# Up-projection of a feed-forward layer by Strassen's seven products, with the other weights streamed through four slots

## The chip, the cores and the metric

The kernel runs on one core of one Trainium2 chip. The metric is the device time of one execution in microseconds (us). TensorE is called PE here, VectorE DVE, ScalarE ACT, GpSimd POOL and the queue of DMA issues on SyncE SP. All arithmetic is fp32; a product of two fp32 matrices is made of three matmuls on a high and a low part of each operand.

## The reference

```python
# x: (32, 128, 512); ctx: (32, 128, 512)
x = x + tanh(g_xattn) * xattn(layernorm(x), ctx)   # 16 heads of 32, k and v from ctx
h = layernorm(x)                                   # 4096 rows of 512
u = square(relu(h @ up_w))                         # up_w: (512, 2048)
s = u @ down_w                                     # down_w: (2048, 512)
r = top_k(h @ gate_w, 2).sum(-1, keepdims=True)    # gate_w: (512, 8)
y = s + (h @ expert_w) * r                         # expert_w: (512, 512)
x = x + tanh(g_ffn) * (norm(y) * gamma + beta)
```

The first layer (attention) is left as it is, but for its last steps; the change is in the second (feed-forward).

## The kernel before

**Tiles.** A row tile is 128 rows of x. After the attention the 32 tiles lie in the DRAM scratch `x2_scratch`. The feed-forward layer takes them in eight groups of four (512 rows); group 0 and group 7 are written out, groups 1 to 6 are the body of one hardware loop (`run`, L1116), with the same order of instructions on each engine in every turn. Nothing plans the order: each engine runs its list in order, and semaphores that only count up (`at_least`) hold it back.

**Splitting.** ACT copies an fp32 tile into a float32r tile (the high part) and DVE or POOL subtracts it from the source (the low part). `mm3` (L68) then issues hi×hi, hi×lo and lo×hi for each of the stationary 128x128 blocks.

**A group.** For each of the 16 output tiles of 128 columns of `up_w`, `upward` (L990) issues 12 matmuls with 512 moving columns (4 blocks of the contraction, 3 each) into bank 4 or 5. ACT takes relu (L1281), DVE squares (L1320), ACT makes the high part (L1272), DVE the low part (L1322), and `downward` (L1220) issues 12 matmuls with 512 moving columns, which add into banks 0 to 3 (`wide`). PE's order is upward(i), downward(i-1). Then come four `expert` products (L1232) of 12 matmuls. `gate` (L1199) and `turn_logits` (L1209) make the routing weights early in the group.

**Weights.** All weights of the layer (up, down, expert) are split once, in group 0, and stay in SBUF. Their tiles carry the names of the attention's weights that lay in the same place: `wk` holds the turned x of the group, `wq` and `up` the up weights, `wv` and `down` the down weights, `wo` the expert weights.

**Turning x.** PE needs x with its 512 features on the partitions. From group 1 on, DVE normalises a tile (L1034), and `deal_blocks` (L1162, on SP) stores it to `xn_scratch` with one DMA (L1164), waits until that has landed, and reads it back with four DMAs (L1169) that permute 32x32 blocks, in pieces of 128 bytes. DVE then transposes inside the blocks (`turn_blocks`, L1010), and ACT and DVE split the result (L1008, L1039). Four tiles a group are so dealt with, each as soon as it is normalised.

**Around it.** `load_x` (L958) fetches the next group's tiles, `finish` (L1182) the residuals and stores the results. The attention's `drain` functions (L253, L396, L578, L739, L863) interleave the last attention tiles with the start of group 0, and `keep_clock` (L339) issues matmuls whose result is not used.

Of the kernel before, what the change touches and what calls it, by code (L numbers as in the profile page):

```python
# [5 lines left out]
F32 = mybir.dt.float32  # L6
# [5 lines left out]
P = 128  # L12
# [11 lines left out]
def flamingo_layer(nc, t, out):  # L24
# [10 lines left out]
    xn_dram = nc.dram_tensor("xn_scratch", [GB, P, D], F32, kind="Internal").ap()  # L35
# [11 lines left out]
    with ExitStack() as whole:  # L47
# [35 lines left out]
        fy = sb(whole, "fy", [P, GB, D])  # L83
        st_x2 = [sem(f"st_x2_{n}") for n in range(2)]
        dv_x2, pe_V = sem("dv_x2"), sem("pe_V")
        ff = feed_forward_start(nc, whole, t, x2_dram, bank, ident, tanh_g, powers, W, fx, fy, at_least, mm3)
# [4 lines left out]
        with ExitStack() as ctx:  # L91
            bk = sb(ctx, "bk", [P, D])
            bq = sb(ctx, "bq", [P, D])
            bv = sb(ctx, "bv", [P, D])
            tgbo = sb(ctx, "tgbo", [P, D])
            nqk = sb(ctx, "nqk", [P, D])
            xin = [sb(ctx, f"xin{n}", [P, D]) for n in range(2)]
            cin = [sb(ctx, f"cin{n}", [P, D]) for n in range(2)]
            xres = [sb(ctx, f"xres{n}", [P, D]) for n in range(2)]
            x2 = [sb(ctx, f"x2_{n}", [P, D]) for n in range(2)]  # L100
            xn = sb(ctx, "xn", [P, D])
            xnT_hi, xnT_lo = sb(ctx, "xnT_hi", [P, D], F32R), sb(ctx, "xnT_lo", [P, D], F32R)
            cT_hi = [sb(ctx, f"cT_hi{n}", [P, D], F32R) for n in range(2)]
            cT_lo = [sb(ctx, f"cT_lo{n}", [P, D], F32R) for n in range(2)]
            kb, qb, vb = sb(ctx, "kb", [P, D]), sb(ctx, "qb", [P, D]), sb(ctx, "vb", [P, D])
            kf, qf = sb(ctx, "kf", [P, D]), sb(ctx, "qf", [P, D])
            junk_k, junk_q = sb(ctx, "junk_k", [P, D]), sb(ctx, "junk_q", [P, D])
            v_hi = [sb(ctx, f"v_hi{n}", [P, D], F32R) for n in range(2)]
            v_lo = [sb(ctx, f"v_lo{n}", [P, D], F32R) for n in range(2)]
            qT_hi, qT_lo = sb(ctx, "qT_hi", [P, D], F32R), sb(ctx, "qT_lo", [P, D], F32R)  # L110
# [4 lines left out]
            pT_hi, pT_lo = sb(ctx, "pT_hi", [P, NG, HG * P], F32R), sb(ctx, "pT_lo", [P, NG, HG * P], F32R)  # L115
            aT = sb(ctx, "aT", [P, NG, P])
# [30 lines left out]
            BO_LAST = bank[6]  # L147
# [54 lines left out]
            def _(sp):  # L202
# [50 lines left out]
                def drain(s, a, o):  # L253
# [5 lines left out]
                    ff.load_piece(sp, ff.nstage)  # L259
                    sp.wait_ge(dv_x2, a + 1)  # L260
                    sp.dma_start(x2_dram[a], x2[a % 2][:, :]).then_inc(st_x2[a % 2], DMA)
                    for m in range(ff.nstage + 1, 2 * ff.nstage):
                        ff.load_piece(sp, m)
# [6 lines left out]
            def _(pe):  # L270
# [125 lines left out]
                def drain(s, a, o):  # L396
# [6 lines left out]
                    ff.turn(pe, 0)  # L403
# [4 lines left out]
                    ff.turn(pe, 1)  # L408
# [3 lines left out]
                    ff.turn(pe, 2)  # L412
                    keep_clock(BO_LAST, 8, 2 * P)
                    keep_clock(BO_LAST, 8, 2 * ff.NE)
                    project_out(a, BO_LAST)
                    turn_probs(s, s % 2, 2)
                    turn_probs(s, s % 2, 3)
                    ff.turn(pe, 3)
                    for g in range(NG):
                        values(s, s % 2, g)  # L420
                    ff.upward(pe, 0, 0)
                    ff.upward(pe, 0, 1)
                    pe.wait_ge(dv_x2, a + 1)
                    project_out(s, BO_LAST)
# [4 lines left out]
            def _(dve):  # L429
# [148 lines left out]
                def drain(s, a, o):  # L578
# [13 lines left out]
                    ff.lo_T(dve, 0, 1)  # L592
                    split_values(a)
# [3 lines left out]
                    ff.piece_lo(dve, 0)  # L597
# [3 lines left out]
                    ff.lo_T(dve, 0, 3)  # L601
                    residual_sum(a, a % 2, BO_LAST)
                    ff.piece_lo(dve, 1)
                    ff.piece_lo(dve, 2)
                    split_values(s)
                    ff.prepare(dve)
                    residual_sum(s, s % 2, BO_LAST)
# [4 lines left out]
            def _(act):  # L612
# [71 lines left out]
                def slot(s, par):  # L684
# [50 lines left out]
                    if is_slot(s, 0):  # L735
                        for k in range(KT):
                            weight_hi(3, k)

                def drain(s, a, o):  # L739
                    hi_v(s, s % 2)  # L740
                    exps(s, s % 2, 0)
                    exps(s, s % 2, 1)
# [737 lines left out]
```

## Time and profile before

| | |
|---|---|
| median of 3 runs | 1479.23 us (1478.67 to 1479.96) |
| the profiled execution | 1478.99 us |
| its span, first to last instruction | 1476.8 us |
| busy: PE, PEld, DVE, ACT, POOL | 98%, 79%, 59%, 46%, 31% |
| mean granted TensorE clock | 0.995 |

The span leaves out what lies before the first and after the last instruction, 2.2 us here. PE is the matmuls, PEld the loads of their stationary operand, which run beside them. A matmul's record is longer than the step to the next one, since matmuls overlap in the array: what a matmul costs is read from the distance of two starts, not from its duration. SPq is SP's queue of DMA issues: a row's time is the time that issuing takes, and the landing of the data comes later. In the timeline, merged rows (x2, x4) run from the start of the first to the end of the last.

### The profile page before, as it was taken

The numbers are of one execution on the slowest core, as the hardware profiler recorded it, in microseconds if no ns is written. First come the engines' busy times: TensorE is split into PE (matmuls) and PEld (weight loads), VectorE is DVE, ScalarE is ACT, GpSimd is POOL, SyncE is SP. The second block draws the span as 40 slices with busy tenths as digits, with TensorE's granted clock in tenths as the row PEclk, the third lists the DMA queues.
The fourth block names the chain that finished last, engine by engine and source line by source line (L and its number), as shares of the span: only waits on it lengthen the run. The fifth ranks groups of instructions, "written<-read, shape, count | busy, mean of one in ns | idle before, by whom it ended". The sixth has DMA issues, their size and how long they took to land.

```text
span 1476.8 us, 24473 instructions
## 1 busy us (share of the span) xinstructions
PE 1444.6 (98%) x7984; PEld 1169.9 (79%) x7984; DVE 869.9 (59%) x1495; ACT 685.8 (46%) x1951; POOL 456.3 (31%) x587
## 2 busy tenths in 40 slices
PE   6899999999999999999999999999999999999997
PEld 4688888888888888778878878788788788788786
DVE  5677777787777788655554353353453443543524
ACT  3677777777777777744322222222222222222221
POOL 2555555555555557600020020020020110200211
PEclk9999999999999999999999999999999999999999
DMA  6121111111111131033411301202211212112000
GB/s 215 44 58 57 57 57 57 57 57 57 55 54 54 51 122 50 30 114 111 124 51 43 87 28 43 71 28 51 63 43 43 64 43 50 56 43 57 36 22 29
DMA packets 103559, 89.74 MB, mean 61 GB/s; under 512 B 64480, under 2 KB 64608, under 8 KB 103520
## 3 DMA queue, kind: packets, MB, share of 16 engines
q1 hardware_dynamic: 102944, 88.19, 20.0%
q10 hardware_dynamic: 576, 1.05, 0.2%
q8 instruction: 22, 0.36, 0.1%
q14 instruction: 17, 0.14, 0.0%
HBM read 65.10 MB, written 24.12 MB: 60 GB/s over the span
## 4 chain that ended last, share of the span: by engine, by line
PE 93%; DVE 2%; POOL 2%; ACT 1%; issue 1%; DMA 1%; SPq 0%; POOLq 0%; DVEq 0%; ACTq 0%
PE bank L74 18%; PE bank L76 17%; PE bank L75 17%; PE wide L74 10%; PE wide L75 10%; PE wide L76 10%; PE bank L324 3%; PE wide L302 3%; PE bank L285 3%; POOL prob L804 1%; ACT prob L636 1%; DMA prob<-in_wk 1%; PE bank L1216 1%; PE bank L1206 0%; PE bank L1203 0%
## 5 line engine op out<-in xcount | busy, mean ns | idle before, releaser
L1281 ACT ACTIVATE relu<-bank 128x512 f32<-128x512 f32 x128 | 76.5, 597 | 420.9 <-PE bank L76 420.9
L1320 DVE TENSOR_TENSOR hid<-relu 128x512 f32<-128x512 f32 x128 | 98.1, 766 | 265.2 <-ACT relu L1281 265.1
L636 ACT ACTIVATE prob<-wide,nmx 128x128 f32<-128x128 f32 x512 | 182.0, 404 | 19.1 <-DVE nmx L458 19.1
L804 POOL TENSOR_TENSOR prob<-prob,rr 128x512 f32<-128x512 f32 x128 | 137.8, 1087 | 88.4 <-DVE rr L466 88.4
L76 PE MATMUL bank<-wk_hi,up_lo 128*128 128x512 f32 x384 | 152.0, 396 | 0.0
L75 PE MATMUL wide<-down_lo,hT_hi 128*128 128x512 f32 x384 | 151.7, 395 | 0.0
L75 PE MATMUL bank<-wk_lo,up_hi 128*128 128x512 f32 x384 | 151.6, 395 | 0.0
L74 PE MATMUL bank<-wk_hi,up_hi 128*128 128x512 f32 x384 | 151.6, 395 | 0.0
L74 PE MATMUL wide<-down_hi,hT_hi 128*128 128x512 f32 x384 | 151.6, 395 | 0.0
L76 PE MATMUL wide<-down_hi,hT_lo 128*128 128x512 f32 x384 | 151.4, 394 | 0.0
L1322 DVE TENSOR_TENSOR hT_lo<-hid,hT_hi 128x512 fp32r<-128x512 f32 x128 | 89.4, 698 | 89.8 <-ACT hT_hi L1272 89.8
L1272 ACT ACTIVATE hT_hi<-hid 128x512 fp32r<-128x512 f32 x128 | 80.9, 632 | 124.1 <-DVE hid L1320 124.1
L636 ACT ACTIVATION_READ_ACCUMULATOR prob<-wide,nmx 128x1 f32 x512 | 125.0, 244 | 0.0
L1067 POOL TENSOR_SCALAR fvar<-fmv 128x1 f32<-128x1 f32 x32 | 7.2, 224 | 332.2 <-DVE fmv L1030 332.2
L1404 POOL TENSOR_TENSOR fres<-fres,beta 128x512 f32<-128x512 f32 x32 | 42.9, 1345 | 179.9 <-DMA fres<-x_scratch 179.9
L614 ACT ACTIVATE aT<-wide 32x512 f32<-32x512 f32 x128 | 75.5, 590 | 42.5 <-PE wide L76 41.0
L614 ACT ACTIVATE pT_hi<-bank 128x512 fp32r<-128x512 f32 x128 | 72.3, 671 | 36.3 <-PE bank L324 36.3
L1398 POOL TENSOR_SCALAR yvar<-ymv 128x1 f32<-128x1 f32 x32 | 15.8, 494 | 227.7 <-DVE ymv L1343 227.7
L75 PEld LDWEIGHTS wide<-down_lo,hT_hi 128*128 128x128 f32 x384 | 72.1, 188 | 17.6
L74 PEld LDWEIGHTS wide<-down_hi,hT_hi 128*128 128x128 f32 x384 | 72.1, 188 | 17.4
L76 PEld LDWEIGHTS wide<-down_hi,hT_lo 128*128 128x128 f32 x384 | 72.1, 188 | 17.4
L75 PEld LDWEIGHTS bank<-wk_lo,up_hi 128*128 128x128 f32 x384 | 72.1, 188 | 17.3
(162 smaller groups left out, 3612.6 us busy)
## 6 DMA issues: line engine op xcount, KB each, us to landing
xin<-in_x SPq DMA_DIRECT2D x32, 256.0 KB, 2.6
cin<-in_ctxT SPq DMA_DIRECT2D x32, 256.0 KB, 2.9
xres<-in_x SPq DMA_DIRECT2D x32, 256.0 KB, 3.5
x_scratch<-x SPq DMA_DIRECT2D x32, 256.0 KB, 2.9
fx<-x_scratch SPq DMA_DIRECT2D x32, 256.0 KB, 2.7
fres<-x_scratch SPq DMA_DIRECT2D x32, 256.0 KB, 3.6
out_x<-fres SPq DMA_DIRECT2D x32, 256.0 KB, 2.0
xn_scratch<-fx SPq DMA_DIRECT2D x28, 256.0 KB, 2.0
```

The source lines that it names most:

```text
L74: eng.matmul(dst, ah, bh, start=first and k == 0, stop=False)
L75: eng.matmul(dst, ah, bl, start=False, stop=False)
L76: mm = eng.matmul(dst, al, bh, start=False, stop=last and k == n - 1)
L285: mm = pe.transpose(cols(dst, k), cols(src, k), ident[:, :])
L302: mm = pe.matmul(cols(bank[g], h), cols(q, h)[strip(g), :], kT[strip(g), m, h, :], start=n == 0, stop=n == 2)
L614: return act.activation(dst, src, ACT.Copy)
L636: i = act.activation(prob[par][:, g, h * P:(h + 1) * P], cols(bank[g], h), ACT.Exp, bias=nmx[:, n:n + 1], scale=1.0, accum_out=rs[:, n:n + 1])
L804: pool.tensor_tensor(p, p, r, ALU.mult).then_inc(po_p, 1)
L1272: return act.activation(dst, src, ACT.Copy)
L1281: act.activation(ff.relu[:, :], bank[4 + i % 2], ACT.Relu).then_inc(ff.ac_r, 1)
L1320: dve.tensor_tensor(ff.hid[:, :], ff.relu[:, :], ff.relu[:, :], ALU.mult).then_inc(ff.dv_h, 1)
L1322: dve.tensor_tensor(ff.hT_lo[i % 2][:, :], ff.hid[:, :], ff.hT_hi[i % 2][:, :].bitcast(F32), ALU.subtract).then_inc(ff.dv_l, 1)
```

## The change

Two output tiles of `up_w` (a pair q of eight) and the group's 512 rows are seen as 2x2 blocks of 256x256 and 256 rows. Strassen's scheme (Winograd's form) gives the 2x2 product with seven half-size products in place of eight. Each of the seven is 6 matmuls with 256 moving columns (2 blocks of the contraction, 3 each). Their operands are sums and differences of blocks: of the weights, made once in group 0 by POOL (`up_sums`), and of the normalised x, made in each group by POOL (`x_sums`) as four more tiles "t" beside the four of x. So eight tiles are dealt, turned and split per group and not four. DVE puts the products together (`sum_2`, `sums_all`: seven operations of 256 columns a pair) and squares with one operation a tile (`squares`); relu on ACT is gone, two copies of 256 columns a pair come in.

The seven sums of up weights take 1.75 times their old room, so the down and expert weights no longer stay in SBUF: group 0 splits them and stores both parts (512 KB a tile) to `ring_scratch`, and groups 1 to 7 read them back through four slots. PE takes the slots in the order down 0 to 13, expert 0 to 3, down 14, 15 ("places" 0 to 19); the expert product now runs one contraction block at a time over banks 4 to 7. A slot is loaded again only when the downward or expert step four places before has ended (`pe_R`).

The core of the diff:

```diff
+    def product(pe, q, b, half, a, moving):
+        stat = [tuple(w[q][:, a * H + kk * P:a * H + (kk + 1) * P] for w in (u_hi, u_lo)) for kk in range(2)]
+        mm3(pe, bank[b][:, half * H:(half + 1) * H], stat, moving).then_inc(pe_P, 1)
-        mm3(pe, bank[4 + i % 2], [tuple(w[:, k * P:(k + 1) * P] for w in up[i]) for k in range(KT)],
-            [(xT_hi[:, k, :], xT_lo[:, k, :]) for k in range(KT)]).then_inc(pe_U, 1)
+        at_least(pe, dv_U, n * NC)                      # upward(g, q): seven products
+        product(pe, q, 4, 0, 0, [x_part(kk, 0) for kk in range(2)])
...
+        at_least(pe, ac_P, n * 2 + 1)
+        product(pe, q, 4, 1, 1, [x_part(2 + kk, 0) for kk in range(2)])
+        at_least(pe, dv_U, n * NC + 1)
+        product(pe, q, 5, 1, 5, [t_part(2, kk) for kk in range(2)])
...
+        def ring_ready(g, n):
+            if is_first(g):
+                pe.wait_ge(ff.rl, n + 1)
+            else:
+                per = NS // KT * 2 * DMA
+                at_least(pe, ff.ring_moved[n % KT], g * per + (n // KT + 1) * 2 * DMA)
...
         def group(g):                                   # PE
+            for q in range(NQ):
+                if not (is_first(g) and q == 0):
+                    ff.upward(pe, g, q, (lambda: turn_logits(g)) if q == 1 else None)
+                if q == 0:
...
+                else:
+                    downward(g, 2 * q - 2)
+                    downward(g, 2 * q - 1)
+            if not is_last(g):
+                experts(g)
+            downward(g, NI - 2)
+            downward(g, NI - 1)
...
+        def ring_load(g, n, last=False):                # SP
+            at_least(sp, ff.pe_R, g * NS + (n - KT + 1), apart=True)
+            i = n if last else ff.ring_order[n]
+            for m in range(2):
+                sp.dma_start(ff.ring[n % KT][m].bitcast(F32), ring_dram[i, m]).then_inc(ff.ring_moved[n % KT], DMA)
+        def out_blocks(g, i):
...
+            sp.dma_start(xn_dram[i], src).then_inc(ff.st_n[ff.pair_of(i)], DMA)
+        def in_blocks(g, i):
+            dst_tile = ff.y[i] if i < GB else ff.xn[i - GB]
+            at_least(sp, ff.st_n[ff.pair_of(i)], g * (2 * DMA), apart=True)
+            src = xn_dram[i].rearrange("(c t) (k i d) -> i t k c d", t=HD, k=KT, d=HD)
+            for m in range(HG):
+                dst = dst_tile[m * HD:(m + 1) * HD, :].rearrange("t (k c d) -> t k c d", k=KT, d=HD)
+                sp.dma_start(dst, src[m]).then_inc(ff.ld_t[ff.pair_of(i)], DMA)
...
         def group(g):                                   # SP, for q in range(NQ)
+                if not first and q in (2, 3):
+                    store_out(g - 1, q - 2)
+                    load_res(g - 1, q)
+                if not first and q == 4:
+                    store_out(g - 1, 2)
+                if not first and q > 0 and 2 * q + 2 < (NI if last else NS):
+                    ring_load(g, 2 * q + 2, last)
+                if not last and q in (6, 7):
+                    jj = q - 6
+                    out_blocks(g + 1, 2 * jj)
+                    out_blocks(g + 1, 2 * jj + 1)
+                    out_blocks(g + 1, GB + jj)
+                    out_blocks(g + 1, GB + jj + 2)
+                    in_blocks(g + 1, 2 * jj)
+                    in_blocks(g + 1, 2 * jj + 1)
+                if not first and q > 0 and 2 * q + 3 < (NI if last else NS):
+                    ring_load(g, 2 * q + 3, last)
+                if not last and q in (6, 7):
+                    jj = q - 6
+                    in_blocks(g + 1, GB + jj)
+                    in_blocks(g + 1, GB + jj + 2)
+                if not first and q == 4:
+                    store_out(g - 1, 3)
...
+            elif not last:
+                for n in range(2 * NQ + 2, NS):
+                    ring_load(g, n)
+            if not last:
+                for n in range(KT):
+                    ring_load(g + 1, n)
...
+    def x_sums(pool, g, jj, t_tiles):                   # POOL, into the tiles y
+        at_least(pool, dv_xn, g * GB + 2 * (jj + 1), apart=True)
+        pool.tensor_tensor(ta[:, 0:H], xb[:, 0:H], xa[:, 0:H], ALU.subtract).then_inc(po_t, 1)
...
+            ff.inv_std(pool, g + 1, 1)                  # POOL's group(g)
+            next_sums(g, 0)                             # waits until all four results are stored
+            ff.inv_std(pool, g + 1, 2)
```

In group 0 the ring is filled by DMA, ACT and DVE: SP stores each split tile and then loads the next piece to be split, in the same places of its list as the ring loads above. In the last group nothing is dealt, and the expert weights are read into the place of up weights that are used up. In the drain of the attention eight tiles are transposed by PE in place of four, POOL makes the first sums, and the two `keep_clock` calls there are gone.

## Rows read from the trace of the kernel before

**Rows 1.** The page: span, busy times, chain of waits that ended last

```profile
span 1476.8 us, 24473 instructions
PE 1444.6 (98%) x7984; PEld 1169.9 (79%) x7984; DVE 869.9 (59%) x1495; ACT 685.8 (46%) x1951; POOL 456.3 (31%) x587
PE 93%; DVE 2%; POOL 2%; ACT 1%; issue 1%; DMA 1%; SPq 0%; POOLq 0%; DVEq 0%; ACTq 0%
```

**Rows 2.** Windows (us, busy of each engine with instructions, clock): one group, gate to gate

```profile
850.40:953.70 103.30, 103.30 (x450) 82.74 (x449) 45.65 (x78) 24.99 (x41) 14.13 (x20) 1.00 0.18 51
```

**Rows 3.** Waits of PE from 650 us to the end

```profile
PE bank L74 <- issue: 0.7, 2, 0.3
```

**Rows 4.** Timeline of PE, 512 moving columns (start us, duration us), the first and last of 13

```profile
1001.36 0.39 PE L74 MATMUL bank<-wk_hi,up_hi 128*128 128x512 f32 x1
...
1004.14 0.40 PE L74 MATMUL wide<-down_hi,hT_hi 128*128 128x512 f32 x1
```

**Rows 5.** Timeline of PE, 256 moving columns, read in narrow windows

```profile
627.42 0.40 PE L342 MATMUL bank<-cT_hi 128*128 128x256 f32 x2
627.54 0.40 PE L342 MATMUL bank<-cT_hi 128*128 128x256 f32 x2
627.66 0.40 PE L342 MATMUL bank<-cT_hi 128*128 128x256 f32 x2
```

**Rows 6.** Timeline of PE and PEld: transposes in groups of four, each behind a wait

```profile
625.76 1.04 PE L324 MATMUL bank<-ident,prob 128*128 128x128 f32 x8
626.63 0.60 PE L982 MATMUL bank<-ident,fx 128*128 128x128 f32 x4
625.53 1.02 PEld L324 LDWEIGHTS bank<-ident,prob 128*128 128x128 f32 x8
1001.13 0.19 PEld L74 LDWEIGHTS bank<-wk_hi,up_hi 128*128 128x128 f32 x1
```

**Rows 7.** Timeline of SP's issues: a tile dealt out and in; residual loads

```profile
893.18 0.33 SPq L1164 DMA_DIRECT2D xn_scratch<-fx  x1
895.26 2.64 SPq L1169 DMA_DIRECT2D fx<-xn_scratch  x4
946.71 2.15 SPq L1185 DMA_DIRECT2D fres<-x_scratch  x4
```

**Rows 8.** DMA issues of one group (count, KB each, median us from issue to landing)

```profile
xn_scratch<-fx SPq DMA_DIRECT2D x4, 256.0 KB, 2.0
fx<-xn_scratch SPq DMA_DIRECT2D x16, 64.0 KB, 2.5
fx<-x_scratch SPq DMA_DIRECT2D x4, 256.0 KB, 2.9
fres<-x_scratch SPq DMA_DIRECT2D x4, 256.0 KB, 4.0
```

**Rows 9.** Groups of DVE, ACT and POOL in one group of tiles (busy us, mean ns | idle before)

```profile
L1320 DVE TENSOR_TENSOR hid<-relu 128x512 f32<-128x512 f32 x16 | 12.3, 769 | 33.6 <-ACT relu L1281 33.6
L1322 DVE TENSOR_TENSOR hT_lo<-hid,hT_hi 128x512 fp32r<-128x512 f32 x16 | 11.1, 692 | 11.3 <-ACT hT_hi L1272 11.3
L1034 DVE TENSOR_SCALAR fx<-fx,fmv,frstd 128x512 f32<-128x512 f32 x4 | 2.2, 541 | 0.0
L1281 ACT ACTIVATE relu<-bank 128x512 f32<-128x512 f32 x16 | 9.6, 598 | 55.5 <-PE bank L76 55.5
L1404 POOL TENSOR_TENSOR fres<-fres,beta 128x512 f32<-128x512 f32 x4 | 5.6, 1407 | 27.2 <-DMA fres<-x_scratch 27.2
```

**Rows 10.** Windows behind PE's last matmul; timeline of PE at half clock

```profile
1468.00:1472.00 4.00, 0.51 (x3) 0.09 (x1) 3.83 (x8) 0.69 (x1) 2.04 (x3) 1.00 0.32 123
1472.00:1476.80 4.80, 0.00 (x0) 0.00 (x0) 1.78 (x3) 0.00 (x0) 1.36 (x2) 0.55 0.28 109
13.18 0.63 PE L75 MATMUL bank<-wk_lo,cT_hi 128*128 128x512 f32 x1
13.61 0.63 PE L76 MATMUL bank<-wk_hi,cT_lo 128*128 128x512 f32 x1
```

**Rows 11.** Waits of PE from 613 to 650 us, the change from attention to group 0

```profile
PE wide L74 <- DVE hT_lo L1322: 1.2, 1, 1.2
PE bank L74 <- DVE aT_lo L431: 0.8, 1, 0.8
PE bank L324 <- DVE pT_lo L431: 0.5, 1, 0.5
PE wide L74 <- ACT prob L636: 0.5, 1, 0.5
```

More of the change, by code:

```diff
@@ L1220, in downward @@
         def downward(g, i):
-            if static(g) and g == 0:
-                pe.wait_ge(ff.fl, ff.have("down", i))
+            n = spot(g, i)
+            ring_ready(g, n)
             at_least(pe, ff.dv_l, g * NI + (i + 1))
@@ L1245, in group @@
[L1245 to L1265 removed]
+                pe.wait_ge(ff.ld_e, KT * 2 * DMA)
@@ L1312, in _, with evict @@
-        run(act, group, before)
+            at_least(act, ff.pe_R, (g + 1) * NS - 2)
+            act.activation(ff.y[j], bank[4 + j], ACT.Copy, scale=route[:, j:j + 1]).then_inc(ff.ac_m, 1)
+        def evict(g, j):
+            at_least(act, ff.pe_R, g * NS + NI)
+            at_least(act, ff.st_o[j], g * DMA)
+            copy(ff.y[j], bank[j]).then_inc(ff.ac_m, 1)
+        def group(g):
+            first, last = is_first(g), is_last(g)
+            for q in range(NQ):
+                if q > 1:
+                    hidden_hi(g, 2 * q - 2)
+                    hidden_hi(g, 2 * q - 1)
+                if q == 1:
+                    logits(g)
+                if first and q == 1:
+                    freed(act)
+                if not (first and q == 0):
+                    ff.copy_1(act, g, q)
+                    ff.copy_5(act, g, q)
+                if q == 1:
+                    hidden_hi(g, 0)
+                    hidden_hi(g, 1)
+                if first and q + 2 < NQ:
+                    if q == 1:
+                        freed(act)
+                        stored(act)
+                    ff.up_hi(act, q + 2, 0)
+                    ff.up_hi(act, q + 2, 1)
+                if first:
+                    if q + 2 < NQ:
+                        ff.up_hi(act, q + 2, 2)
+                    ring_hi(2 * q)
+                    ring_hi(2 * q + 1)
+            hidden_hi(g, NI - 2)
+            hidden_hi(g, NI - 1)
+            if last:
+                for j in range(GB):
+                    evict(g, j)
+                return
+            if first:
+                ring_hi(2 * NQ)
+                ring_hi(2 * NQ + 1)
+            for i in range(GB):
+                ff.hi_T(act, g + 1, i)
+            if first:
+                ring_hi(2 * NQ + 2)
+                ring_hi(2 * NQ + 3)
+            ff.hi_T(act, g + 1, GB)
+            ff.hi_T(act, g + 1, GB + 1)
+            weigh(g, 0)
+            ff.hi_T(act, g + 1, GB + 2)
+            weigh(g, 1)
+            ff.hi_T(act, g + 1, GB + 3)
+            weigh(g, 2)
+            weigh(g, 3)
@@ L1427, in after @@
                 scale_y(NGRP - 1, j)
-        run(pool, group, before, after)
+        run(pool, group, None, after)
 def kernel(**inputs):
```

980 lines of the change are left out of this document (646 added, 334 removed).

## The prediction

> **What bounds the kernel now.** I read the page first: PE is busy 98% of the span and carries 93% of the chain that ended last, with DVE at 59% and ACT at 46% [rows 1]. Then I cut out one feed-forward group, from gate to gate. PE is busy for the whole 103.3 us at full clock, DVE for 45.7, ACT for 25.0 and POOL for 14.1 [rows 2], and from 650 us to the end PE waits only 0.7 us [rows 3]. So the layer is a stream of matmuls, and what counts is the step from one to the next and whether anything new interrupts it. With 512 moving columns 12 steps take 2.78 us, 0.232 us each [rows 4]. A group is 440 such matmuls (384 up and down, 48 expert, 8 gate), 102.1 us, and the small ones of the logits. A steady group is thus 103.3 us, and eight are 826 of the 1477 us.
>
> **The matmuls.** The only place that shows 256 moving columns with a new 128x128 stationary block each is a keep-clock burst: starts at 627.42, 627.54, 627.66, 0.120 us apart [rows 5]. A pair of output tiles took 24 x 0.232 = 5.57 us and now takes 42 x 0.120 = 5.04 us. Strassen removes one eighth of the columns, 0.70 us, but 1.75 times as many loads and starts give 0.17 back. Over 8 pairs and 8 groups the gain is 64 x 0.53 = 34 us. Bounds: the transposes, 128 columns with full weight loads, step by 0.109 us (eight of them and the four behind them start 0.87 us apart) [rows 6], so 0.109 is a floor (gain 64 x 0.99 = 63). The records of the loads are 0.19 us long but start closer than that, so 0.19 isn't the step. A ceiling is half of 0.232 plus the excess of a 512 step over 512 columns at 2.4 GHz (0.232 - 0.213 = 0.019), 0.126 (gain 18). I take the burst's 0.120, as it is the same shape. The seven waits of a pair cost nothing when already met: the transposes in rows 6 are groups of four, each behind a wait, without a break.
>
> By the Trainium skill (TensorE: Matmul & The Clock Gate, sections "Back-to-back issue gap" and "LDWEIGHTS") a warm matmul takes 262 cycles at 256 columns and 518 at 512, and a load of 128 columns about 107 ns whatever streams beside it. The trace agrees on the load's floor (0.109) and shows 0.016 more at 512 columns and 0.011 more at 256. By the page's steps the gain would be 64 x (24 x 0.216 - 42 x 0.109), an estimate of 39 us, and a further halving of the columns would gain nothing, since the load would be the step.
>
> **DVE and ACT within a pair.** At 512 columns DVE takes 0.69 to 0.77, ACT 0.60 from PSUM [rows 9]. For 256 columns I halve the part that grows with columns and get 0.42 on DVE and 0.4 on ACT (bounds 0.35 and 0.69, 0.30 and 0.60). DVE adds 7 x 0.42 = 2.9 us a pair, and four more turned tiles a group (transpose 0.7, low part 0.7) 5.6 us: 46 + 24 + 6 = 76 of some 99 us. PE's period is 5.04 + 5.57 = 10.6 us a pair. DVE must hand over the sums within the 5.57 us of the two downwards: from the last product two sums (0.8 us) if it isn't behind. The hidden tiles are needed 10.6 us after the product: two squares, high and low parts, about 4 us. Hidden. ACT loses 16 relus (9.6 us) and gains 16 copies of 256 (6.6 us) and four copies of turned tiles; it is idle three quarters of the group. Nothing.
>
> **One wait that POOL brings.** next_sums(g, 0) needs the four results of the group before stored, and the last store is issued behind ring load 11, so behind downward 7, the end of pair 4. From there: ring load 0.95, store landing 2.0 to 3 [rows 8], four half-width POOL operations 2.8 (half of 1.41 each [rows 9]), the inverse deviation of the third tile, queued behind them on POOL, 0.8, then on DVE normalise 0.54, statistics 1.0 and six sums 2.5. That is 10.6 to 11.9 us, against 10.6 us until PE wants bank 4. DVE's sums of pair 5 stand behind that normalise, and PE behind the sums. 0 to 2.5 us a group; I take 1.3, six times: 8 us.
>
> **The queue of SP at the turn of a group.** Here I expect the result to be decided. Before, four tiles were dealt, each by itself when it was normalised, and nothing that PE needed soon was queued behind them. A deal is 0.33 us of issue, a landing 2.08 us after its start, and four issues of strided DMAs in 2.64 us, 0.67 from start to start; these land 2.5 us after issue [rows 7, 8]. Now eight tiles are dealt in pairs 6 and 7, in one list with ring loads of 512 KB that PE needs within this stretch. Count from the end of downward 10, before which SP may not issue ring load 14, and so nothing behind it. PE, if never held, runs downward 11 (2.78), pair 7 (5.04), downwards 12 and 13 (5.57), expert 0 to 2 (8.35): expert 3, which reads ring load 17, would start at 21.7 us. Before load 17 has been issued SP must issue:
> - 24 strided DMAs (six tiles in) at 0.67 and six waits at 0.15: 17.0 us
> - 16 plain DMAs (loads 14 to 17, eight tiles out) at 0.45, between the 0.33 of a bare one and the 0.6 of those in the loop (four in 2.15 [rows 7]): 7.2 us
> - twice the wait for a landing, 2.08 and 0.5 for the ring load ahead of it, less the 1.3 us in which two more tiles go out: 2.5 us
>
> Together 26.7 us, and the load lands 2.9 us later [rows 8], at 29.6: expert 3 is 7.9 us late (1 us of it already at expert 2). It ends at 32.4. Behind load 17 stand two more tiles in (5.7 us) and load 18 (0.95), which lands at 36.2: downward 14 is another 3.8 us late. Load 19 follows by 0.95 and is hidden by downward 14. Sum 11.7 us. PE's clock: behind its last matmul (1468.5 us) the clock is full until 1472 and 0.55 in the next window; at the start of the kernel matmuls at 1.2 GHz step by 0.43 us [rows 10]. An idle time of 7.9 us is longer than those 4 us, so expert 3 would run at half clock, 2.3 us longer, nearly all inside the wait for load 18. I take 12 us a turn. Bounds: with 0.38 and 0.66 us an issue, no cost for waits, and landings of 2.0 us, load 17 lands at 26.2 and the sum is 7.6 us; with 0.6 and 0.73 and landings of 4 us [rows 8] it is 18.
>
> It would not help to have only the ring right: the last tile in is issued at 32.5 us and lands at 35, then transpose 0.7, high 0.6, low 0.7 make 37, while an undisturbed PE would want the t tiles at 30 + 2.2 = 32. Both chains come from the same list. Six turns (groups 1 to 6): 72 us.
>
> **Group 0.** Its turn has the same eight tiles, but between them SP stores split tiles and loads raw ones that ACT and DVE must still split. All eight deals stand ahead of the load for place 18: the two steps with their stores and loads come to about 37 us, landing 3, split 1.4: downward 14 at 41 against 24.5, and 1 us more behind it in load 19. 17 us (bounds 11 and 22, the spread of the other turns scaled).
>
> **The rest.** In the drain 16 more transposes (1.7 us) and POOL's sums, against two keep-clock bursts (1.7 us) gone and PE waits of 3.0 us there now [rows 11]: +2 (between -3 and +6). The tail after the last matmul keeps its shape: 0. Drained and loaded weights in other groups: ring loads 4 to 13 have over 15 us each, 0.
>
> **Sum**, against the profiled execution's 1479.0 us (span 1476.8 and 2.2 around it; the median of the runs is 0.2 higher): 1479.0 - 34 + 8 + 72 + 17 + 2 = 1544 us. All low ends together give 1479 - 63 + 0 + 46 + 11 - 3 = 1470, all high ends 1479 - 18 + 15 + 108 + 22 + 6 = 1612; they won't fall together, and the likeliest case's own range is 1502 to 1580.
>
> **Rivals.**
> 1. The list of SP is not in the way: stores and strided issues overlap more than rows 7 show, and the turn costs at most what POOL's and DVE's chain costs. For it: SP is hardly used in the rest of the group, PE has four slots ahead, and a reader of rows 3 sees that the old deals held nobody. Against: SP's starts 0.67 apart are in the trace, inside the same loop. Then 1479 - 34 + 2 + some 3 = 1450, faster. It decides from a stall of under 4.9 us a turn (34 over 7). 11%.
> 2. The stall is there but small, 4 to 5.5 us a turn (the plain DMAs cheap, E3 alone late): 1479 - 34 + 7 x 4.75 + 2 = 1480, between 1475 and 1502. 7%.
> 3. The half-width step isn't 0.120: the load, 0.19 us by its record, becomes the step when it meets a wait or a fresh bank. 42 x 0.19 = 8.0 us a pair, 64 x 2.4 = 154 us more than now, and with longer pairs the turn's stall falls to some 9 us: 1479 + 154 + 63 = 1696. The burst and the transposes speak against it. 2%.
> 4. The change doesn't do what it says: PE gains nothing since the products' seven waits break the stream (the step behind a real wait is about 0.1 us longer): 64 x 7 x 0.08 = 36 us, the gain is gone: 1580. Within the upper end; 5%.
>
> **Chances.** Likeliest case 75%. The range 1490 to 1575 leaves out rivals 1 and 3, most of rival 2 and part of rival 4, some 2 in 10. A measurement tells 0.2%, 3 us, from no change: faster 0.12 (rival 1 and a part of 2), same 0.01, slower 0.87.
>
> **What would show it.** PE steps of 0.120 in the seven products (right: 0.118 to 0.126). In each group from 1 to 6 two idle times of PE, some 7 us ahead of the third or fourth expert block and some 4 ahead of downward 14, both released by the DMA of the ring; SP's queue without a hole from downward 10 to there, mostly strided issues; the clock at half right behind the longer one. Group 0 longer than the others by 5 us at its turn. A wait of about 1 us ahead of pair 6, ended by DVE. Wrong, if the groups are 99 us long, if PE's waits at the turn are ended by DVE's low parts of x alone, or if the steps are 0.19.

## The result, and the profile of the changed kernel

The changed kernel takes 1613.06 us, the median of 4 runs (1611.13 to 1616.2), against 1479.6 of the kernel before beside it (1478.67 to 1480.04): a ratio of 1.0905, 95% interval 1.0885 to 1.0924. Forecast were 1544 us in a range of 1490 to 1575. The sign and the places are as predicted; the time is outside the range. The profiled execution took 1616.2 us, 3 above the median.

Its span is 1614.4 us. Three lines of the page (busy times, clock in 40 slices, chain of waits), against [rows 1]:

```profile
PE 1464.2 (91%) x9136; PEld 1236.7 (77%) x9136; DVE 1090.9 (68%) x2003; ACT 679.8 (42%) x1991; POOL 557.8 (35%) x691
...
PEclk9999999999999999888799899899899899898999
...
PE 65%; SPq 12%; DMA 8%; DVE 7%; issue 4%; POOL 3%; ACT 1%; POOLq 0%; DVEq 0%; ACTq 0%
```

SP's queue and the DMAs now hold 20% of the chain that ended last, where they held 1%. PEclk falls to 8 and 7 in four slices around group 0, and then dips in about every third slice: once a group. PE is busy for 20 us more although it has less to do, so part of it runs slower. The windows (us, busy time of each engine with instructions, granted clock, DMA share, GB/s) of group 0, gate to gate, and of groups 1 to 6 with some 1.6 us behind them, against [rows 2]:

```profile
647.20:810.60 163.40, 120.93 (x593) 102.43 (x592) 97.04 (x155) 44.11 (x81) 49.29 (x46) 0.83 0.51 157
810.60:1512.70 702.10, 629.34 (x3563) 541.07 (x3561) 429.91 (x848) 140.57 (x270) 122.67 (x170) 0.94 0.53 154
```

From one gate to the next, group 0 takes 163.4 us (before: 102.2), and groups 1 to 6 take 115.7, 114.7, 118.3, 116.4, 118.3 and 117.0 (before: 103.2 to 103.8). The sum of differences is whole: 2.3 us up to the first gate, 61.2 in group 0, 79.8 in groups 1 to 6 and -5.7 behind them make 137.6, the difference of the spans.

What PE waits for (us in total, times, longest), first in group 0, then from 815 to 1512 us, which is groups 1 to 6. Before there was nothing to see here [rows 3]:

```profile
PE wide L75 <- DVE wo_lo L1716: 10.0, 1, 10.0
PE bank L75 <- DVE c L1286: 7.9, 5, 2.4
PE bank L75 <- DVE c L1307: 7.8, 4, 2.8
PE bank L75 <- DVE wo_lo L1716: 7.7, 1, 7.7
PE bank L75 <- ACT c L1270: 5.8, 5, 1.2
PE wide L1552 <- ACT lg L1618: 3.3, 1, 3.3
```

```profile
PE bank L75 <- DMA wo_lo<-ring_scratch: 50.9, 12, 6.6
PE wide L75 <- DMA wo_lo<-ring_scratch: 11.2, 6, 2.4
PE bank L75 <- DVE c L1307: 10.7, 6, 2.1
```

In groups 1 to 6 three waits a group are for a ring load: 12 ahead of expert blocks (`bank`), 6 ahead of downward 14 (`wide`). One more a group is for DVE's sums. In group 0 two long waits (7.7 and 10.0 us) for the low part of a ring tile stand at its turn, and 14 short ones, which the prediction did not have, inside its pairs.

The steps of PE (start, duration) in the products and at the turn of group 1, with the wait and its releaser in brackets:

```profile
879.34 0.28 PE L75 MATMUL bank<-wk_hi,up_hi 128*128 128x256 f32 x1
879.46 0.28 PE L76 MATMUL bank<-wk_lo,up_hi 128*128 128x256 f32 x1
...
898.29 0.80 PE L75 MATMUL bank<-wo_hi,wk_hi 128*128 128x512 f32 x1 [2.76 <-DMA wo_lo<-ring_scratch]
...
909.34 0.79 PE L75 MATMUL bank<-wo_hi,wk_hi 128*128 128x512 f32 x1 [6.59 <-DMA wo_lo<-ring_scratch]
...
913.77 0.63 PE L76 MATMUL bank<-wo_lo,wk_hi 128*128 128x512 f32 x1
914.20 0.63 PE L77 MATMUL bank<-wo_hi,wk_lo 128*128 128x512 f32 x1
915.50 0.50 PE L75 MATMUL wide<-wo_hi,hT_hi 128*128 128x512 f32 x1 [0.67 <-DMA wo_lo<-ring_scratch]
```

The step at 256 columns is 0.12 us (0.118 as the median of some 2600 of them), a little under the 0.120 of [rows 5]. Expert 2 starts at 898.3 and expert 3 at 909.3, both behind a wait. The first seven steps of expert 2 and all of expert 3 are at half clock: the granted clock is 0.50 from 898.3 to 901.4 and from 909.4 to 914.5, which is 1.2 GHz, and the steps there are 0.43 us (the first one 0.59). From its first start to its last expert 2 takes 4.1 us and expert 3 4.9, instead of 11 × 0.232 = 2.6.

SP's issues in the same stretch (start, duration, count). Downward 10 ends at about 876.8, and the list goes on; the ring loads at 876.80, 887.26, 894.50 and, with its second half, 905.63 are those of places 14 to 17, `xn_scratch<-` is a tile dealt out, `<-xn_scratch` two tiles in:

```profile
876.80 0.32 SPq L1425 DMA_DIRECT2D wo_hi<-ring_scratch  x1
...
877.82 0.80 SPq L1433 DMA_DIRECT2D xn_scratch<-fy  x2
881.70 5.37 SPq L1441 DMA_DIRECT2D fy<-xn_scratch  x8
887.26 0.47 SPq L1425 DMA_DIRECT2D wo_hi<-ring_scratch  x1
...
888.33 5.98 SPq L1441 DMA_DIRECT2D fx<-xn_scratch  x8
894.50 0.48 SPq L1425 DMA_DIRECT2D wo_hi<-ring_scratch  x1
...
899.59 5.33 SPq L1441 DMA_DIRECT2D fy<-xn_scratch  x8
905.63 0.43 SPq L1425 DMA_DIRECT2D wo_lo<-ring_scratch  x1
```

This is the list that the prediction counted out, without a hole but for the waits for the landing of what was dealt out. Load 17 has been issued 29.3 us after the end of downward 10 (906.06 against 876.8; forecast 26.7), and expert 3 starts 32.5 us after it (forecast 29.6). So nearly all of the delay is time before the issue; from the end of the issue to the start of expert 3 it is only 3.3 us.

### The profile page after: what moved, and what is told of

Its sections match the earlier page's. It is cut to its first block, busy times and chain, and to the rows that moved or that the text cites. A ratio compares the mean times of both kernels' runs of the same rounds, so it can differ in the third digit from the quotient of the medians.

```text
span 1614.4 us, 28988 instructions
## 1 busy us (share of the span) xinstructions
PE 1464.2 (91%) x9136; PEld 1236.7 (77%) x9136; DVE 1090.9 (68%) x2003; ACT 679.8 (42%) x1991; POOL 557.8 (35%) x691
## 4 chain that ended last, share of the span: by engine, by line
PE 65%; SPq 12%; DMA 8%; DVE 7%; issue 4%; POOL 3%; ACT 1%; POOLq 0%; DVEq 0%; ACTq 0%
PE bank L75 12%; PE bank L77 11%; PE bank L76 11%; SPq L1441 9%; PE wide L75 7%; PE wide L76 7%; PE wide L77 7%; DMA xn_scratch<-fy 3%; PE bank L326 3%; PE wide L304 3%; PE bank L287 2%; SPq L1425 2%; DMA fy<-in_up 1%; DMA wo_lo<-ring_scratch 1%; DVE c L1313 1%
## 5 line engine op out<-in xcount | busy, mean ns | idle before, releaser
L75 PE MATMUL wide<-wo_hi,hT_hi 128*128 128x512 f32 x512 | 208.3, 407 | 21.1 <-DMA wo_lo<-ring_scratch 11.2
L76 PE MATMUL wide<-wo_lo,hT_hi 128*128 128x512 f32 x512 | 208.1, 406 | 0.0
L77 PE MATMUL wide<-wo_hi,hT_lo 128*128 128x512 f32 x512 | 206.4, 403 | 0.0
L75 PEld LDWEIGHTS wide<-wo_hi,hT_hi 128*128 128x128 f32 x512 | 100.1, 195 | 46.7 <-issue 14.3
L75 PE MATMUL bank<-wq_hi,up_hi 128*128 128x256 f32 x384 | 111.4, 290 | 7.9 <-DVE c L1286 7.9
L77 PEld LDWEIGHTS wide<-wo_hi,hT_lo 128*128 128x128 f32 x512 | 99.3, 194 | 24.0
L76 PEld LDWEIGHTS wide<-wo_lo,hT_hi 128*128 128x128 f32 x512 | 99.8, 195 | 21.3
L76 PE MATMUL bank<-wq_lo,up_hi 128*128 128x256 f32 x384 | 110.5, 288 | 0.0
L77 PE MATMUL bank<-wq_hi,up_lo 128*128 128x256 f32 x384 | 110.3, 287 | 0.0
L1313 DVE SCALAR_TENSOR_TENSOR c<-c 128x512 f32<-128x512 f32 x128 | 97.4, 801 | 0.0
```

What stands on the lines that cost most here:

```text
L75: eng.matmul(dst, ah, bh, start=first and k == 0, stop=False)
L76: eng.matmul(dst, ah, bl, start=False, stop=False)
L77: mm = eng.matmul(dst, al, bh, start=False, stop=last and k == n - 1)
L1313: dve.scalar_tensor_tensor(out=cc[:, m, :], in0=cc[:, m, :], scalar=0.0, in1=cc[:, m, :], op0=ALU.max, op1=ALU.mult).then_inc(dv_h, 1)
```

## The experiments

The theory, T1: the changed kernel is slow because urgent ring loads stand in SP's in-order list behind deals, and in group 0 also because loads of up pieces stand there behind stores that wait for DVE. The rival, T2: the DMA engines themselves are the bound, since the layer now moves 154 GB/s where it moved 51 [rows 2]; then it doesn't matter which queue issues. Each run is set against the kernel before on the same chip (medians 1479.65 to 1479.99).

**e1: the late ring loads on ACT's queue.** Of the changed kernel, loads 14 to 19 of groups 1 to 6 are issued by ACT between its copies of hidden tiles and of turned x, the first four each behind the `hidden_hi` of one tile, the last two behind the copies (`hi_T`) of the second and the fourth turned tile (not in this cut of the diff):

```
+        def act_load(n):
+            for m in range(2):
+                act.dma_start(ff.ring[n % KT][m].bitcast(F32), ring_dram[ff.ring_order[n], m]).then_inc(ff.ring_moved[n % KT], DMA)
...
             hidden_hi(g, NI - 2)
+            if mid:
+                act_load(NX + 2)
```

> The ring loads for places 14 to 19 in groups 1 to 6 are issued on ACT's queue, each behind the copy that has waited for the same step of PE; the deals of the turned tiles stay on SP, and the same 16 DMA engines move the same bytes. Theory 1, the order in SP's list holds the loads back: PE's waits ahead of expert 2, expert 3 and downward 14 (2.3, 6.2 and 2.1 us in the changed kernel) are gone, the clock stays full there, and what is left is a wait for the turned t tiles at the start of the next group, some 4 us, since SP still has eight deals in a row: a turn costs 4 to 5 us and not 14.7, so about 60 us less, 1550 us. Theory 2, the DMA engines are full with the 128-byte pieces: the loads land as late as before and the time falls by less than 10 us.

Measured: 1541.29 us (1537.2 to 1546.99, 4 runs), 1.043 (1.0403 to 1.0457). The same bytes go by another queue, and 72 us are gone. Groups 1 to 6 take 101.8 to 107.6 us. PE's waits between 800 and 1440 us:

```profile
PE wide L75 <- DMA wo_lo<-ring_scratch: 12.5, 6, 4.2
PE bank L75 <- DVE c L1307: 11.5, 7, 2.0
PE bank L75 <- ACT fy L1643: 1.7, 3, 0.7
```

The waits ahead of the expert blocks are gone. Those ahead of downward 14 remain, up to 4.2 us long: they are for load 18, which stands in ACT's list behind copies of turned tiles. In group 1 these waited 9.7 us for tiles that SP was still dealing, and only then was load 18 issued:

```profile
900.35 0.33 ACTq L1653 DMA_DIRECT2D wo_hi<-ring_scratch  x1
```

Downward 14 starts at 905.05. The expectation had put what is left at the start of the next group instead. The wait that POOL's order brings is unchanged.

**e2: plain reads in place of the strided ones.** The four strided DMAs that read a dealt tile become one plain DMA of the same bytes. The permutation of the 32x32 blocks is left out.

```
-            for m in range(HG):
-                dst = dst_tile[m * HD:(m + 1) * HD, :].rearrange("t (k c d) -> t k c d", k=KT, d=HD)
-                sp.dma_start(dst, src[m]).then_inc(ff.ld_t[ff.pair_of(i)], DMA)
+            sp.dma_start(dst_tile, xn_dram[i]).then_inc(ff.ld_t[ff.pair_of(i)], DMA)
```

> Each dealt tile is read back with one plain DMA of 256 KB in place of four with 128-byte pieces: the 32x32 blocks are not permuted, so the up and expert products get wrongly ordered features. Everything else stays, the place of all ring loads in SP's list too. Theory 1: 24 issues of 0.67 us stood ahead of load 17, six plain ones of 0.45 take their place, load 17 is issued some 13 us earlier, and the turn's waits of groups 1 to 6 (14.7 us with the half clock) go altogether; so does part of group 0's 18 us: 1613 - 88 - 10 = 1515 us. Theory 2 (the engines' bandwidth): the same direction, but less, since the bytes are the same: some 40 us.

Measured: 1509.3 us (1506.38 to 1511.37, 4 runs), 1.0198 (1.0181 to 1.0214); groups 100.9 to 102.3 us, group 0 148.6. Of the 134 us lost, 104 go with the 64 KB pieces. What remains between 800 and 1440 us:

```profile
PE bank L75 <- DVE c L1307: 12.0, 7, 2.0
PE bank L75 <- DMA wo_lo<-ring_scratch: 3.0, 4, 1.1
```

By itself this doesn't tell whether the pieces cost SP's time or the DMA engines'; e1 and e6 do, which leave the pieces as they are.

**e3: group 0's up pieces ahead of the ring stores.** In SP's list of group 0 two loads of pieces of `up_w` are issued two steps earlier, ahead of the stores that wait for DVE:

```
+                ff.load_piece(sp, p + 6)
+                ff.load_piece(sp, p + 7)
                 ring_store(2 * q)
                 ff.load_piece(sp, p + 4)
                 ring_store(2 * q + 1)
-                for n in range(5, 8):
-                    ff.load_piece(sp, p + n)
+                ff.load_piece(sp, p + 5)
```

> Only group 0: SP loads the two up pieces of pair q+3 ahead of the ring stores of pair q, not behind them. Theory 1: the pairs of group 0 take 17 us since they are a closed loop: low parts of the ring tiles (DVE), stores and loads on SP, landing 4.4 us, split of the up pieces, and only behind that DVE's sums, squares and again the low parts. With the loads some 5 us earlier each of pairs 2 to 6 takes 12 to 13 us: 20 to 25 us less, 1590 us. Theory 2: DVE's own work bounds the pair (squares 1.7 us each beside POOL): the pairs stay at 16 to 17 us and the time within 5 us.

Measured: 1591.04 us (1590.02 to 1591.77, 4 runs), 1.0753 (1.0737 to 1.0769); group 0 137.3 us in place of 163.4. PE's waits inside the pairs (660 to 752 us) and at the turn (752 to 815):

```profile
PE bank L75 <- DVE c L1286: 3.7, 3, 1.7
PE bank L75 <- DVE c L1307: 2.0, 3, 1.0
```

```profile
PE bank L75 <- DVE wo_lo L1717: 11.2, 1, 11.2
PE wide L75 <- DVE wo_lo L1717: 10.9, 1, 10.9
```

The 21.5 us of short waits have become 5.7; the turn is no better (22.1 us of waits in place of 17.7). So the pairs of group 0 were held by the place of two loads in a list.

**e4: POOL's order.** The inverse deviation of the third tile goes ahead of the sums that wait for the stores of results:

```
             ff.inv_std(pool, g + 1, 1)
-            next_sums(g, 0)
             ff.inv_std(pool, g + 1, 2)
+            next_sums(g, 0)
             ff.inv_std(pool, g + 1, 3)
```

> POOL makes the inverse deviation of the third tile before the sums of x that wait for the stored results, not behind them. Theory 1: PE's wait of 2.0 us ahead of pair 6 in groups 1 to 6, released by DVE's sums of pair 5, goes, with the half clock behind it: 12 us less, 1601 us. Theory 2: another wait stands right behind (the x sums then come later against the deals): 0 to 3 us less.

Measured: 1601.65 us (1598.11 to 1602.1, 5 runs), 1.0816 (1.0801 to 1.0831), 11.4 us less than the changed kernel. PE's waits between 800 and 1440 us have no row of DVE's `c` any more:

```profile
PE bank L75 <- DMA wo_lo<-ring_scratch: 47.4, 10, 7.9
...
PE wide L75 <- DMA wo_lo<-ring_scratch: 8.2, 5, 2.3
```

**e5: e3, and the low parts of the up sums on DVE.** POOL no longer makes `up_lo_sums` beside DVE's squares; DVE makes them behind the squares. It is to be compared with e3:

```
-                    ff.up_lo_sums(pool, q)
...
                     ff.squares(dve, g, q)
+                if first and q + 2 < NQ:
+                    ff.up_lo_sums(dve, q + 2)
```

> To be compared with e3_up_first (1591 us): in group 0 the low parts of the summed weights (1024 columns) are made by DVE behind its squares and not by POOL beside them. Theory 1: the two squares take 1.75 us each in group 0 against 0.65 in the other groups only because POOL's subtraction runs at the same time; without it they take 0.65 to 0.8, DVE gains 2 us and pays 1.2 for the moved operation: pairs 2 to 5 some 1 us shorter, 3 to 5 us less, 1587 us. Theory 2: the squares are slow for another reason (tiles loaded by DMA at the same time): they stay at 1.7 us and the pair gets longer by 1.2 us, 1596 us.

Measured: 1583.61 us (1579.38 to 1586.25, 4 runs), 1.07 (1.0679 to 1.0721); group 0 132.6 us. DVE's squares (L1313) and one of its sums (L1303), both with two operands in SBUF, between 655 and 740 us (count, busy us, mean ns). The squares in the changed kernel, then both in e3, then both here:

```profile
L1313 DVE SCALAR_TENSOR_TENSOR c<-c 128x512 f32<-128x512 f32 x10 | 17.3, 1773 | 0.0
```

```profile
L1313 DVE SCALAR_TENSOR_TENSOR c<-c 128x512 f32<-128x512 f32 x14 | 10.7, 800 | 0.0
L1303 DVE TENSOR_TENSOR c<-c 128x256 f32<-128x256 f32 x7 | 9.6, 1378 | 0.2
```

```profile
L1313 DVE SCALAR_TENSOR_TENSOR c<-c 128x512 f32<-128x512 f32 x14 | 10.1, 765 | 0.0
L1303 DVE TENSOR_TENSOR c<-c 128x256 f32<-128x256 f32 x7 | 3.4, 484 | 0.2
```

The squares were already down to 0.80 us in e3, where POOL still makes its subtraction: with the new order it falls on DVE's sums instead, and one of these takes up to 2.5 us. The gain that the expectation put on the squares comes from the sums. Only with the subtraction off POOL are both short. DVE has more to do in this version and gets through it sooner. That is worth 4.7 us in group 0 and 7.4 in the whole time, after e3.

**e6: all ring loads on ACT's queue.** e3 and e4, and every ring load of groups 1 to 7 is issued by ACT two tiles ahead, behind the hidden tile of its number:

```
+        def hidden_load(g, i):
+            hidden_hi(g, i)
+            if not is_first(g) and i + 2 < (NI if is_last(g) else NX + KT):
+                act_load(g, i + 2)
```

> e3 and e4 together, and all ring loads of groups 1 to 7 on ACT's queue, each behind the copy that has waited for the same step of PE; SP's list holds the deals with nothing ahead of them. Theory 1 (two lists that blocked each other in one queue): in groups 1 to 6 the deals of the first pair start when POOL's sums are ready, at pair 6, the turned tiles are there before PE wants them, and no wait over 1 us is left: 99 to 101 us a group. 1613 - 22 (group 0's pairs) - 12 (POOL's order) - 6 x 14.7 = 1491 us. Theory 2 (ACT's issues, 0.35 to 0.45 us each and 40 a group, hold up its own copies in turn): 104 us a group, as in e1, 1515 us.

Measured: 1484.45 us (1482.47 to 1486.94, 8 runs), 1.0032 (1.0022 to 1.0043). Groups 1 to 6 take 99.1 to 99.6 us. All that PE waits for between 800 and 1440 us is

```profile
PE bank L75 <- ACT fy L1649: 3.0, 6, 0.8
```

while SP's deals go on undiminished, some of the strided ones even slower, up to 7.4 us for eight:

```profile
859.91 7.44 SPq L1441 DMA_DIRECT2D fx<-xn_scratch  x8
```

Nobody waits for them, because the ring is no longer behind them. This decides against T2: the bytes and pieces are those of the changed kernel, in groups 17 us shorter. The Trainium skill (DMA: Bandwidth & Descriptors, section "Rules for kernel authors") says that spreading DMAs over issuing engines gives no bandwidth and only saves the sequencer's issue time. That fits: what the urgent loads escaped here is the issuing, and the waiting for landings, of the deals ahead of them in SP's list.

**e7: group 0's turn as well.** e6, and the stores and loads for ring places 12 to 19 of group 0 are issued by ACT, each behind the low part it waits for; places 18 and 19 are split before the last turned tiles:

```
+        def act_move(n):
+            act.wait_ge(ff.rl, n + 1)
+            for m in range(2):
+                act.dma_start(ring_dram[ff.ring_order[n], m], ff.ring[n % KT][m].bitcast(F32)).then_inc(ff.ring_moved[n % KT], DMA)
+            if n + 2 < NS:
+                ff.load_piece(act, ff.r_at[n + 2])
```

> e6, and in group 0 the stores and loads of the ring for the places 12 to 19 on ACT's queue too, so that SP has only the deals there. Theory 1: PE's two waits for the ring's low parts at the turn of group 0 (11 and 11 us in e3, with half clock behind them) shrink to the time that two staging buffers need (load 3, split 1.4, each second one): under 5 us in all, some 20 us less than e6: 1471 us, a little under the kernel before. Theory 2: the staging buffers alone set these waits: 5 us less than e6 at most.

Measured: 1470.93 us (1470.43 to 1472.92, 5 runs), 0.9944 (0.993 to 0.9958). Group 0 takes 125.5 us; one wait of 8.3 us ahead of downward 14 is left of the two of 11, and 1.3 us in two short ones.

**e8: all of it.** e7 with e5's move, and ACT issues the first two loads of the next group behind the last `weigh`:

```
             ff.hi_T(act, g + 1, GB)
-            if not first:
-                act_load(g, 0)
-                act_load(g, 1)
...
             weigh(g, 3)
+            if not first:
+                act_load(g, 0)
+                act_load(g, 1)
```

> e7, and with it e5 (the low parts of the summed weights on DVE) and one move in groups 1 to 6: ACT issues the first two ring loads of the next group behind the last weighing of the expert product, not ahead of it. Theory 1: the 0.86 us step of PE at the start of each of the groups 2 to 7 (PE waits 0.5 us for ACT's fourth weighing) goes, 3 us, and group 0 loses 4 to 5 us, as from e3 to e5: 1471 - 7 = 1464 us. Theory 2: group 0 is held by the staging of the ring at its end, which takes back what its pairs gain: 1468 us.

Measured: 1465.23 us (1464.36 to 1468.47, 4 runs), 0.9895 (0.988 to 0.991): 1% faster than the kernel before. Groups 3 to 6 take 98.6 us each, group 0 121.4. The busy times of its page (span 1466.7 us), and a window of 100 us in the steady groups:

```profile
PE 1416.5 (97%) x9136; PEld 1208.9 (82%) x9136; DVE 1087.1 (74%) x2009; ACT 681.9 (46%) x1991; POOL 543.9 (37%) x685
```

```profile
855.00:955.00 100.00, 98.09 (x590) 85.70 (x589) 72.42 (x141) 23.50 (x45) 20.22 (x28) 1.00 0.67 178
```

PE does the same 9136 matmuls as in the changed kernel in 48 us less busy time, since the clock is full in the groups behind group 0, and the DMA engines carry 178 GB/s instead of 154.

**e9: the kernel before with half-width matmuls.** To price the step by itself: `upward` of the kernel before issues each of its 12 matmuls of 512 columns as two of 256, 24 in all.

```
-        mm3(pe, bank[4 + i % 2], [tuple(w[:, k * P:(k + 1) * P] for w in up[i]) for k in range(KT)],
-            [(xT_hi[:, k, :], xT_lo[:, k, :]) for k in range(KT)]).then_inc(pe_U, 1)
+        for half in range(2):
+            c = slice(half * (D // 2), (half + 1) * (D // 2))
+            mm = mm3(pe, bank[4 + i % 2][:, c], [tuple(w[:, k * P:(k + 1) * P] for w in up[i]) for k in range(KT)],
+                     [(xT_hi[:, k, c], xT_lo[:, k, c]) for k in range(KT)])
+        mm.then_inc(pe_U, 1)
```

> The kernel before, with its up-projection's matmuls split in two halves of 256 columns each, on the same data: 24 matmuls of 256 for 12 of 512 a tile, nothing else. It prices the half-width step with everything else at rest. 128 tiles: with steps of 0.118 us (as in the changed kernel) 128 x (24 x 0.118 - 12 x 0.232) = 6 us more, 1485 us; with 0.126 31 us more; with 0.109, the floor of the weight loads, 21 us less.

Measured: 1486.32 us (1484.45 to 1487.09, 5 runs), 1.0039 (1.0026 to 1.0053). PE's steps:

```profile
1000.18 0.28 PE L74 MATMUL bank<-wk_hi,up_hi 128*128 128x256 f32 x1
1000.30 0.28 PE L75 MATMUL bank<-wk_lo,up_hi 128*128 128x256 f32 x1
```

24 times 0.118 is 0.05 us more than 12 times 0.232; over 128 tiles that is 6 us, and 6.3 were measured. So two matmuls of 256 columns with fresh weights cost hardly more than one of 512, and Strassen's eighth is not eaten by its 1.75 times as many loads: 0.61 of its 0.70 us a pair is left.

## Why the prediction missed

The terms of its sum, with what they measured. The yardstick for a group without stalls is e8's 98.6 us, against 103.3 before. (e8 has the same stream of matmuls.)

| term | forecast, us | measured, us |
|---|---|---|
| matmuls, 8 groups | -34 | -38 (8 × 4.7) |
| stalls of groups 1 to 6 | +80 (72 + 8) | +108 (79.8 + 6 × 4.7) |
| stalls of group 0 | +17 | +66 (61.2 + 4.7) |
| start of the layer, and behind group 6 | +2 | +1.3 (2.3 up to the gate; behind group 6, -5.7 + 4.7 = -1.0) |
| sum on the profiled execution | 1544 | 1616.2 (0.4 less around the span) |

Of the 72 us between 1544 and 1616, group 0 has 49 and groups 1 to 6 have 28; the matmuls give 4 back.

**Right: the matmuls.** 0.118 us a step instead of 0.120, the burst's step [rows 5]. It stands 0.009 us above the 0.109 that the Trainium skill gives for 256 columns (TensorE: Matmul & The Clock Gate, section "Back-to-back issue gap"): the measurement decides. The page gives that figure for an isolated matmul, which the prediction did not say; its estimate of 39 us from the page's figures lies beside the 38 measured. The seven waits of a pair do not break the stream when they are met (rival 4), and there is no step of 0.19 (rival 3).

**Right in mechanism and place: the turn in groups 1 to 6.** Idle time behind expert blocks and downward 14, released by the ring; SP's queue full from downward 10 on; the count of its issues exact. e1 shows the cause, with nothing changed but the queue of the late loads, and e6 confirms it. Rival 1, that the list is not in the way, would have given groups of about 99 us.

**A size that was off: the clock behind the wait.** PE's waits for the ring are 62.1 us in groups 1 to 6, 10.4 a group, where 11.7 were forecast; the idle part was a little over the mark. But a group loses 18.0 us in all: 10.4 for the ring, 1.8 ahead of pair 6, and 5.8 that are no waits, nearly all of them work at half clock. The prediction said that expert 3 "would run at half clock, 2.3 us longer, nearly all inside the wait for load 18". It had compared the idle time with the 4 us for which the clock stayed full behind the last matmul [rows 10]. In fact expert 2 is held first, and a wait of 2.8 us is followed by half clock too; and load 18 is not late enough to hide what expert 3 loses. In group 1 expert 2 loses 1.5 us by it and expert 3 2.3. The 5.8 us are the remainder over all six groups, and the window above with its clock of 0.94 bears them out: 6% of 117 us is 7 us, a part of which falls into idle time. The clock took 5.8 us where 0.3 was allowed: some 33 us over six groups, more than all that these groups took over the forecast.

**A size that was off: the wait ahead of pair 6.** 1.6 to 2.1 us a group instead of 1.3. The terms that the prediction lists for it add to 10.6 to 11.6 us, not to 11.9, so they give 0 to 1.0 us and not up to 2.5. POOL's first sum and DVE's normalise in group 1 (start, duration, idle time before it in brackets):

```profile
860.71 0.73 POOL L1218 TENSOR_TENSOR fy<-fx 128x256 f32<-128x256 f32 x1 [10.04 <-DMA out_x<-fy]
...
864.64 0.55 DVE L1238 TENSOR_SCALAR fx<-fx,fmv,frstd 128x512 f32<-128x512 f32 x1 [6.51 <-POOL frstd L1245]
```

The last store was issued at 857.30 and landed 3.4 us later, beside ring traffic, rather than in the lower part of the 2.0 to 3 us allowed. The chain is the one predicted; with POOL's order changed the wait is gone (e4).

**Failed: group 0.** The step that failed is the one headed "Group 0", 17 us with bounds of 11 and 22, with the word "Hidden" ahead of it, which had priced DVE and ACT for the steady pair alone. Group 0 lost 66 us. The view of its waits above divides it: 17.7 us of waits at its turn, about what was forecast; 21.5 in its pairs; 3.3 ahead of `turn_logits` (ACT's `lg`); the other 23 are the half clock: what PE's steps outside the waits take beyond 0.118 and 0.232 us adds up to 22 (the mean clock is 0.83, and 17% of 163.4 is 28, idle time included). A pair took up to 17 us instead of 10.6. Four engines go round in a loop there. First DVE (start, duration):

```profile
687.28 3.49 DVE L1313 SCALAR_TENSOR_TENSOR c<-c 128x512 f32<-128x512 f32 x2
...
699.58 1.58 DVE L1183 TENSOR_TENSOR up_lo<-fy,up_hi 128x512 fp32r<-128x512 f32 x2 [6.07 <-ACT up_hi L1170]
```

then SP's queue and ACT:

```profile
691.39 0.33 SPq L1419 DMA_DIRECT2D ring_scratch<-wo_hi  x1
...
694.32 1.24 SPq L1041 DMA_DIRECT2D fy<-in_up  x2
```

```profile
698.91 0.64 ACT L1170 ACTIVATE up_hi<-fy 128x512 fp32r<-128x512 f32 x1 [6.93 <-DMA fy<-in_up]
```

DVE's squares end at 690.8, its low parts of the ring follow; only then may SP store the ring tiles (691.39), and only behind four stores and two loads does it issue the two up pieces (694.32). They land 4.4 us later, ACT splits them, DVE makes their low parts at 699.58, 6 us after it last had anything to do, and PE's sums stand behind that in DVE's order. Then the squares start again. Nothing in the loop is overloaded; DVE is busy 59% of the group (97.0 of 163.4 us). The time is in the order. Two loads moved up in one list took 26 us off the group (e3), POOL's subtraction given to DVE 4.7 more (e5), the turn on another queue 11 more (e7 over e6: 136.8 to 125.5). The prediction had written down that SP stores and loads between deals in group 0, but worked that out for the turn alone.

With the half clock hardly priced and a loop in group 0 not worked out, the bounds were too narrow as well: they scaled group 0 from the other turns, which have no such loop.

**Slips that decide nothing.** The ceiling of the half-width step, 0.126, is 256 columns at 2.4 GHz (0.107) and 0.019; half of 0.232 and 0.019, as the prediction words it, would be 0.135. Sixteen copies of 0.4 us are 6.4 us, not 6.6.

**Not settled.** Group 0 of e8 still takes 121.4 us against 98.6, with one wait of 8.5 us for the ring at its turn, 3.3 ahead of `turn_logits`, and a clock of 0.93. Whether a better order there would give the rest was not tried.

## What to carry to other kernels

When a change puts more work into an in-order queue, write the queue out and count what stands ahead of each urgent item: this gave the stall of the middle groups to within 1.3 us of idle time. Do this for every group whose list differs, the first above all, where staging adds its own items; that an engine is idle 40% of the time says nothing about a loop through several of them. And price an interruption of the matmuls as its idle time plus the half clock behind it, here 5.8 us for 12 us of waiting. The cure was free here: move the urgent loads to an issue queue in which nothing long stands ahead of them, ACT's. And when a reordering is to be priced, compare an operation's time with the run just before it: an overlap can move to another operation, as POOL's subtraction did in e3.

## What the runs showed of the hardware

- **DVE beside POOL.** DVE operations whose operands both lie in SBUF take longer where POOL's subtraction reads SBUF beside them: two squares 3.49 us instead of 1.29 in the changed kernel, one sum of 256 columns 2.51 us instead of 0.43 in e3 (at 697.28, beside a subtraction of 2.56 us at 696.95). With the subtraction off POOL (e5) the means are 0.77 us for a square and 0.48 for the sum. The two squares of 3.49 us start at 687.28; POOL's subtraction over 1024 columns lies within:

```profile
687.58 2.63 POOL L1207 TENSOR_TENSOR up_lo<-pair,up_hi 128x1024 fp32r<-128x1024 f32 x1 [1.17 <-ACT up_hi L1176]
```

  The Trainium skill has the rule (SBUF — State Buffer, section "Who interferes with whom"): a DVE instruction with two SBUF inputs contends with a GpSimd instruction that reads SBUF, and one of them blocks. The trace agrees: two squares alone take 1.29 us (at 868.53), here 2.2 us more, most of POOL's 2.63. Moving this work from POOL to the busier engine made it shorter as well: 2.5 us on POOL, 1.2 on DVE.
- **Half clock.** Waits of 2.8 and 6.6 us were each followed by a granted clock of 0.50 and steps of 0.43 us at the turn. From 915.50 on the clock is 1.00 and the step is back at 0.23 to 0.34. Group 0 as a whole had a clock of 0.83.
- **Strided issues.** Eight strided DMAs of 64 KB take SP 5.3 to 6.0 us, 0.67 to 0.75 each, and up to 0.93 in e6, where ACT's queue issues ring loads beside them (most there are as before, and whether ACT's issues are the cause is not shown), against 0.3 to 0.5 for a plain one of 256 KB on either queue. The landing of a tile dealt out rose from 2.0 us [rows 8] to 3.4 and 3.8.
